# Waiting for seven of nine gathers instead of all nine, before GpSimd issues the next group

## The reference

```python
v00 = gather(y0i, x0i); v01 = gather(y0i, x1i)
v10 = gather(y1i, x0i); v11 = gather(y1i, x1i)
out = v00*(1-wx)*(1-wy) + v01*wx*(1-wy) + v10*(1-wx)*wy + v11*wx*wy
attn = softmax(einsum('bgpc,bgpkc->bgpk', qh, k))   # over the 9 samples
out = einsum('bgpk,bgpkc->bgpc', attn, v)           # then a projection, and x is added
```

## Time and profile before

| | |
|---|---|
| three runs | 10973.56, 10989.29 (median), 10993.63 us |
| the profiled execution, its own time | 10980.76 us |
| its span on the chip | 10979.0 us |
| TensorE busy, share of the span | 7942.1 us, 72% |
| VectorE busy | 5184.5 us, 47% |
| ScalarE busy | 3774.6 us, 34% |
| GpSimd busy | 5030.1 us, 46% |
| granted TensorE clock, mean | 0.85 |

### The profile page before, as it was taken

The page is one execution under the profiler, slowest core; times in us unless marked ns, Lnnn a source line. Parts: engine busy times, 40 slices in busy tenths (PEclk is TensorE's granted clock), DMA queues, the critical chain, the costliest instruction groups (busy, mean ns, idle before and its releaser), DMA issues. The chain is left out here.

```text
span 10979.0 us, 96354 instructions
## 1 busy us (share of the span) xinstructions
PE 7942.1 (72%) x31522; PEld 4244.0 (39%) x31522; DVE 5184.5 (47%) x10029; ACT 3774.6 (34%) x5495; POOL 5030.1 (46%) x4864
## 2 busy tenths in 40 slices
PE   7635554642686378876888867688588979998699
PEld 3623222442343144333443433343344434444366
DVE  7432323544454355554655545455454346663233
ACT  2100001300253045442555543255255625552132
POOL 1065655555566656665665666566564000000322
PEclk9867776875898689887998888798799979998799
DMA  3824334565443344434434334443443121104221
GB/s 122 315 83 114 102 100 142 174 205 164 144 126 94 124 126 123 117 111 135 123 116 124 109 114 141 148 127 103 146 118 92 34 83 47 54 19 131 95 78 53
DMA packets 658544, 1283.57 MB, mean 117 GB/s; under 512 B 189043, under 2 KB 398218, under 8 KB 643408
## 3 DMA queue, kind: packets, MB, share of 16 engines
q0 software_dynamic: 234240, 639.57, 19.2%
q1 hardware_dynamic: 405392, 562.58, 17.2%
q10 hardware_dynamic: 18432, 75.51, 1.7%
HBM read 1003.44 MB, written 278.91 MB: 117 GB/s over the span
## 5 line engine op out<-in xcount | busy, mean ns | idle before, releaser
L664 POOL DMA_INDIRECT sa_slot<-s_table,sa_rec x4608 | 4773.1, 1036 | 3610.2 <-DMA sa_slot<-s_table,sa_rec 1554.8
L1654 DVE CUSTOM_DVE_ANT_0 a_above<-a_late,a_above 128x512 f32<-128x512 f32 x1600 | 1102.7, 689 | 1696.8 <-PE a_late L1506 1030.3
L1561 PE MATMUL a_ctx<-a_p,a_v 128*64 128x512 f32 x6400 | 1669.8, 645 | 102.6 <-issue 101.6
L1595 ACT ACTIVATE a_above<-a_diff 128x512 f32<-128x512 f32 x1600 | 956.5, 598 | 2270.6 <-PE a_diff L1494 1268.8
L1586 ACT ACTIVATE a_p<-a_s 128x1024 f32<-128x1024 f32 x1600 | 1629.2, 1021 | 179.8 <-PE a_s L1544 123.2
L710 DVE TENSOR_TENSOR sa_slot<-sa_slot,sa_q 128x1152 f32<-128x1152 f32 x512 | 694.1, 1356 | 1728.3 <-DMA sa_slot<-s_table,sa_rec 1710.6
L1506 PE MATMUL a_late<-a_k,a_q 96*128 96x512 f32 x1600 | 831.4, 520 | 426.0 <-DVE a_pair_max L1654 355.3
L819 PE MATMUL sa_sums<-keep_ident,sa_vals 128*128 128x128 f32 x4608 | 688.6, 299 | 589.0 <-DVE sa_vals L762 586.7
L1494 PE MATMUL a_diff<-a_kd,a_q 96*128 96x512 f32 x1600 | 745.9, 466 | 506.7 <-DMA a_q<-s_q 434.6
L1544 PE MATMUL a_s<-a_q,a_k 98*128 98x512 f32 x3200 | 1079.5, 422 | 30.8 <-ACT a_p L1586 30.6
L819 PEld LDWEIGHTS sa_sums<-keep_ident,sa_vals 128*128 128x128 f32 x4608 | 616.4, 157 | 686.3 <-DVE sa_vals L762 606.9
(11 more groups left out here) (280 smaller groups left out, 8150.5 us busy)
## 6 DMA issues: line engine op xcount, KB each, us to landing
sa_slot<-s_table,sa_rec POOLq DMA_INDIRECT x4608
s_table<-t_rows ACTq DMA_DIRECT2D x64, 1024.0 KB, 7.5
a_q<-s_q SPq DMA_DIRECT2D x480, 128.0 KB, 2.5
s_part<-a_o SPq DMA_DIRECT2D x160, 256.0 KB
t_qwin<-s_dwq SPq DMA_DIRECT2D x64, 512.0 KB
t_kvwin<-s_dwkv SPq DMA_DIRECT2D x64, 386.0 KB
a_kd<-s_kd SPq DMA_DIRECT2D x384, 64.0 KB
a_o<-s_part SPq DMA_DIRECT2D x96, 256.0 KB, 2.6
```

What stands on the lines that cost most here:

```text
L664: pool.indirect_dma_start(out=self.slot[g][:, k, :, :, :].rearrange("p c a n -> p (c a n)"), out_offset=None, in_=self.s["table"][n // TIL ...
L1561: mm = pe.matmul(self.ps_ctx[i * 2 * HD:(i + 1) * 2 * HD, :], self.v_and_ones(run.head, kb), self.p[slot % P_SLOTS][:, i * CHUNK:(i + 1) * ...
L1595: act.activation(self.above[slot % n][:, :], self.ps_diff, ACT.Relu).then_inc(self.diff_got, 1)
L1654: dve.tensor_tensor_reduce(above, self.ps_late, above, 1.0, LOWEST, ALU.add, ALU.max, self.pair_max[:, t, j:j + 1]).then_inc(self.late_got, 1)
```

## The change

GpSimd's wait ahead of a group asks for the first seven of the nine gathers of the group ahead of it. The last two gathers of each group add to a semaphore of their own, `gathered_late[g]`, and VectorE, which needs all nine, waits for both semaphores ahead of its first instruction on the group. Nothing else is touched: the same gathers go out in the same order.

```diff
+EARLY = 7
@@ Sampling.__init__
         self.gathered = [r.sem(f"gathered{g}") for g in range(G)]
+        self.gathered_late = [r.sem(f"gathered_late{g}") for g in range(G)]
@@ Sampling.gather
         if G * n + g > 0:
             before = G * n + g - 1
-            pool.wait_ge(self.gathered[before % G], 16 * K * (before // G + 1))
+            pool.wait_ge(self.gathered[before % G], 16 * EARLY * (before // G + 1))
         for k in range(K):
             pool.indirect_dma_start(
...
-            ).then_inc(self.gathered[g], 16)
+            ).then_inc(self.gathered[g] if k < EARLY else self.gathered_late[g], 16)
@@ Sampling.q_times_k
-        dve.wait_ge(self.gathered[g], 16 * K * n + 16 * K)
+        dve.wait_ge(self.gathered[g], 16 * EARLY * (n + 1))
+        dve.wait_ge(self.gathered_late[g], 16 * (K - EARLY) * (n + 1))
```

## The result

| | before | after |
|---|---|---|
| median of the runs | 10991.5 us (10973.6 to 11004.2, 4 runs) | 9918.7 us (9907.4 to 9936.2, 4 runs) |
| profiled execution's span | 10979.0 us | 9914.7 us |
| mean granted clock of TensorE | 0.85 | 0.884 |

The ratio is 0.9026, with an interval of 0.9008 to 0.9045: 1073 us are gone. The forecast was 10440 us, a gain of 540, with a range down to 10250.

What follows compares the result with a forecast made beforehand. GpSimd was taken to hold itself back, waiting for its own gathers to land. Gains of 333 us (three stages) and 220 us (others), less 13 us, made 540 us off 10980.8: 10440 us, range 10250 to 10700.

Steps and rivals of the forecast that it cites:

- The gap: GpSimd between groups: idle 2.82 us falls to the plain 0.30 us, 2.5 us less per group.
- The three stages of the earlier trace: Second image's maps, tables and first project stage: 133 landing waits x 2.5 us, all reaching the end, 333 us.
- The other stages: Attention and the remaining stages: VectorE's 550 us of waits, 80% removed and half turning into time, 220 us.
- The factor 0.5: Attention: share of a vanished VectorE wait that becomes time, taken between 0.8 and 0.4 from three 250 us stretches.
- The base of 550 us: VectorE's waits outside the three stages, 1710.6 - 1160.5 us, taken as the most those other stages could yield.
- Rival (b): Attention: VectorE's waits turn fully into time, 333 + 550 = 883 us gained, 10100 us; chance 0.12.
- The added wait: VectorE's second wait before its first instruction on a group: costs 10 us, between 0 and 154 us.
- The issue beside VectorE: Gather issues lengthened beside two-input VectorE instructions: 415 us already, extra cost nothing; 45 us worse if GpSimd never pauses.
- (a): Uneven landings save 1.25 us per group and TensorE binds attention: 276 us gained, 10705 us; chance 0.18.
- (c): GpSimd's issues lengthen with up to eleven gathers in flight, making the kernel slower: 11250 us; chance 0.04.
- (d): Gathers land in bunches, the seventh with the ninth, so GpSimd starts no earlier: 10980 us; chance 0.03.
- What would show it: Expected trace signs: landing waits some 350 us, first-stage period 12.5 us, last gather near 7880, TensorE 85% in attention.

Runs made afterwards that it cites:

- the slow kernel: The best kernel with gathers placed 2 pieces, not 15, behind the piece that frees their slot in the written order: 12680.6 us, ratio 1.1506.
- the split kernel: The changed kernel with GpSimd waiting for both semaphores, so all nine gathers of the group ahead: 11008.4 us; repeated in more rounds, ratio 1.0031.
- the best kernel: The changed kernel with GpSimd waiting for all nine gathers of the group before the last instead of seven of the last: 9665.7 us, ratio 0.8824.
- 10 pieces: The best kernel with gathers placed 10 pieces, not 15, behind the piece that frees their slot in the written order: 12542.6 us, ratio 1.1378.

## Why the prediction was wrong

**The gap: right.** 2.82 us were to become 0.30. In the first stage they became 0.75, the median over all groups is 0.36 us (2.83 before), and the landing waits fell to 388.2 us, forecast some 350.

**The three stages of the earlier trace rows: right.** 333 us were forecast and 365 came, in the stretches that hold them. GpSimd still set the pace there, with a period of 11.89 us where 12.5 was expected.

**The other stages: this step failed.** It offered 332 waits x 2.5 = 830 us, and let 550 x 0.8 x 0.5 = 220 us through; 699 us came, 0.84 of the offer. Two factors were at fault.

The factor 0.5, what a wait in attention is worth, should have been about 1: 569 us of loop for 579 us of waits in the table above. It came from TensorE's busy time in three stretches of 250 us, 6% less in the second and 5% in the third. But the clock stood at 0.96, 0.91 and 0.90 there, and a matmul at the lower level is busy for longer (the late matmul 0.80 us against 0.50 in the slow kernel's trace), which hides the loss. The same hold what doesn't hide it: 941, 837 and 845 matmuls, and ScalarE busy for 145.02, 128.73 and 127.27 us. By ScalarE's work 11% and 12% of a stretch was lost, 28 and 31 us, beside 20.9 and 35.3 us of wait.

The base of 550 us, VectorE's waits on gathers in the trace before, is no ceiling. The attention loop from 2893 us has none of them in that trace and was shortened by 64 us; all seven loops have 288 us of them and were shortened by 540. The two profiles of the split kernel show why: such waits came to 579 us in its loops in one and to 145 in the other, at the same time. In the profile before part of the loss stands before the maximum of attention, behind matmul results that came late; why it stands there stays open.

What should have been compared were periods. The long attention loop holds 92 groups. In the best kernel, where gathers hold nobody, it took 1153 us, 12.5 us per group, and the first loop of the kernel before gave an estimate of it, 2.51 us per slot x 4.87 slots a group = 12.2 us. GpSimd's period before was longer, 15.4 us for the mean of all, so TensorE did not set the time. That estimate was not safe, though: the second loop, also without waits for gathers in that trace, ran at 2.86 us per slot. After the change 9 x (1.044 + 0.305) = 12.1 us stands beside it: both are about even, and the best kernel gained in attention only 26 us more.

**The clock.** In the second to fourth attention loops the clock stood at its lower level for 99, 175 and 264 us before and for 53, 85 and 92 us after. Without the stretch at the lower level with which each loop begins it is 72, 143 and 229 us, and 7, 24 and 17. The prediction's factor had no term for it. What it cost can't be read off: the loops lost what VectorE waited for gathers, one to one, so little is left for the clock. It is argued, not shown, that while GpSimd sets the pace a longer matmul only fills time in which TensorE would stand idle. Rival (b), waits in attention turning fully into time, is what happened; it had 0.12 and gave 10100 us, since its cap of 550 us was the same wrong base. With 699 in its place it would have given 10981 - 333 - 699 = 9949 us.

**The added wait:** 10 us, between 0 and 154, were forecast; the split kernel paid some 30 us (0.3%), GpSimd's second wait included.

**The issue beside VectorE.** 1223 gathers overlapped a q times k or a values instruction before and 1533 after. What they took above 0.946 us came to 392 and 426 us; all issues together took 39 us more. The prediction took nothing for this and named 45 us for a GpSimd that never pauses. The Trainium skill (SBUF — State Buffer, "Who interferes with whom") says that a VectorE instruction with two SBUF inputs contends with a GpSimd instruction that reads SBUF. The trace agrees: the mean issue beside one took 1.267 us before, the others 0.95.

**Rivals.** (a), half of it lost because TensorE binds, fell: attention gave the larger part. (c), slower issues, fell: 1.045 us with up to 18 in flight. (d) fell. **What would show it:** the landing waits and the first stage's period came near their forecasts, the last gather came at 7386 us and not near 7880, TensorE went to 92% in the long attention loop and not to 85%. The forecast of new waits for freed slots and barriers, "several hundred", was wrong: 80.4 and 170.5 us. GpSimd hardly ran into full slots, since VectorE kept up with it. The forecast line "I am wrong if attention stages shorten by as much as their waits" is what happened.

## What to carry to other kernels

To ask whether a side stream sets the time of a busy stage, compare its period with the main engine's need per period. A busy share of 84% and short waits of the consumer say little: the consumer's waits came to 2073.8 and 1590.1 us in two profiles of one kernel, and a lower clock swells the busy share. Count instructions, or take the busy time of an engine whose instructions last the same in both kernels (ScalarE's exponential took 1.02 us in each).

Where an engine waits for its own transfers only to limit what is in flight, wait for older ones: all nine of the group before the last was 2.2% faster than seven of the last by the two ratios (0.8824 and 0.9026). It was run with the split semaphores; it doesn't need them, but that was not run. Moving a producer forward in the order once it has a lead went with a kernel 30% slower than the best by the two ratios (1.1506 against 0.8824), on another chip: look at the stands and the late results before you do it.

## What the runs showed of the hardware

- An indirect gather costs GpSimd about 1.0 us of issue and 0.30 us between issues, whether it brings 1 KB or 256 bytes to a partition (1.034 and 1.010 us), and with nine or with eighteen in flight.
- When GpSimd stood for some 40 us and then issued 36 gathers on end, TensorE's results reached their readers up to 28.9 us late (chips 0 and 9). With stops of 2.8 us behind every nine, on the same chip 9, none of 1600 reached VectorE over 5 us late, against 111 without the stops and with 10 pieces. Results 1 to 5 us late came in profiles of chips 0 and 9 and of the kernel before, and in none of chips 1 and 5. The cause was not found.
- In three attention loops the stretches at 1.2 GHz, those at each loop's start left out, came to 444 us before and 48 after, while TensorE's idle time in the longest of them fell from 212 to 96 us.
- The same program, profiled on two chips at times 0.15% apart, showed 2073.8 and 1590.1 us of one engine's waits for gathers: where idle time stands is not a property of the program alone.
